# The maxima of the attention scores, reduced over two PSUM banks at a time

## The reference

```python
scores = einsum('bhqd,bhkd->bhqk', q, k) * scale     # 16 heads, 128 x 128 each
attn = softmax(scores, axis=-1)
y = einsum('bhqk,bhkd->bhqd', attn, v)
```

## Time and profile before

| what | us |
|---|---|
| median of 3 runs | 760.41 (759.85 to 762.28) |
| the profiled execution | 765.32 |
| its span, from first to last instruction | 763.6 |
| PE busy in the span | 687.0 (90%) |
| DVE busy in the span | 458.2 (60%) |
| all 256 reductions of line 576, busy | 164.3 |

### The profile page before, as it was taken

The page is one execution under the profiler, slowest core; times in us unless marked ns, Lnnn a source line. Parts: engine busy times, 40 slices in busy tenths (PEclk is TensorE's granted clock), DMA queues, the critical chain, the costliest instruction groups (busy, mean ns, idle before and its releaser), DMA issues. The chain is left out here.

```text
span 763.6 us, 19550 instructions
## 1 busy us (share of the span) xinstructions
PE 687.0 (90%) x6885; PEld 522.2 (68%) x6885; DVE 458.2 (60%) x1267; ACT 437.5 (57%) x679; POOL 299.6 (39%) x491
## 2 busy tenths in 40 slices
PE   5888999999969599899999999784899999997997
PEld 5646666666657377799999999771666666665553
DVE  6676887776654322533333444464899987775663
ACT  4346888888834133244444444452688889884442
POOL 5664545441142773573005720046766232112110
PEclk8979999999999899999999999996999999997999
DMA  6686665444112512133123331267454344400011
GB/s 206 103 147 105 133 131 115 103 103 74 36 31 63 199 45 70 49 108 93 55 70 88 108 94 40 68 145 139 106 121 123 83 77 82 69 2 1 29 42 42
DMA packets 72405, 66.77 MB, mean 87 GB/s; under 512 B 8159, under 2 KB 63352, under 8 KB 72056
## 3 DMA queue, kind: packets, MB, share of 16 engines
q1 hardware_dynamic: 57800, 51.88, 30.3%
q0 software_dynamic: 4096, 8.40, 3.9%
q10 hardware_dynamic: 10416, 5.25, 2.5%
HBM read 21.55 MB, written 16.65 MB: 50 GB/s over the span
## 5 line engine op out<-in xcount | busy, mean ns | idle before, releaser
L576 DVE TENSOR_REDUCE a_negmax<-psum 128x4 f32<-128x512 f32 x256 | 164.3, 684 | 7.0 <-PE psum L690 6.3
L443 ACT ACTIVATE temp<-psum 128x1024 f32<-128x1024 f32 x128 | 131.0, 1024 | 19.4 <-PE psum L708 13.2
L690 PE MATMUL psum<-a_k_stack,a_q_stack 96*128 96x256 bf16 x512 | 84.5, 283 | 6.2 <-DVE a_negmax L576 4.5
L722 PE MATMUL psum<-temp,a_v_st 128*18 128x128 f32 x2048 | 81.2, 275 | 7.2 <-issue 3.1
L1393 PE MATMUL psum<-f_w,f_h 128*128 x624 | 87.4, 284 | 0.0
L1380 PEld LDWEIGHTS psum<-f_bxT,f_bw 128*128 128x128 f32 x624 | 82.6, 193 | 6.5 <-issue 3.7
L1380 PE MATMUL psum<-f_bxT,f_bw 128*128 128x128 f32 x624 | 83.1, 277 | 3.3 <-DVE f_bw L1245 3.3
L1051 ACT ACTIVATE f_h<-psum 128x512 f32<-128x512 f32 x78 | 46.6, 597 | 62.2 <-PE psum L1380 62.2
L1245 DVE COPY f_bw<-f_w 128x512 f32 x78 | 34.1, 437 | 79.2 <-PE psum L1380 79.2
L708 PE MATMUL psum<-a_q_stack,a_k_stack 128*128 128x128 bf16 x1024 | 80.1, 222 | 0.7 <-ACT temp L443 0.3
L377 POOL CAST a_nm_cols<-a_negmax 128x16 bf16<-128x16 f32 x64 | 13.6, 212 | 170.9 <-DVE a_negmax L576 170.7
(11 more groups left out here) (204 smaller groups left out, 1258.2 us busy)
## 6 DMA issues: line engine op xcount, KB each, us to landing
a_k_stack<-a_k_parts SPq DMA_DIRECT2D x192, 64.0 KB
a_q_stack<-a_q_parts SPq DMA_DIRECT2D x96, 128.0 KB
xs<-zeros ACTq DMA_DIRECT2D x8, 640.0 KB, 5.2
f_w<-in_f_w SPq DMA_DIRECT2D x18, 256.0 KB, 4.5
scratch<-xs SPq DMA_DIRECT2D x18, 256.0 KB, 3.3
ys<-f_y_out SPq DMA_DIRECT2D x18, 256.0 KB, 2.3
scratch<-in_ctx SPq DMA_DIRECT2D x16, 256.0 KB
x<-in_x SPq DMA_DIRECT2D x8, 256.0 KB, 6.1
```

The costliest lines, as they stand in the source:

```text
L443: nc.scalar.activation(pt[:, unit].rearrange("p a b t -> p (a b t)"), ps[:, bank:bank + 2].rearrange("p a n -> p (a n)"), ACT.Exp, scale=S ...
L576: nc.vector.tensor_reduce(negmax[:, b % 2, :, 2 * unit:2 * unit + 2].rearrange("p n b -> p b n"), ps[:, P1_BANK + unit % 2].rearrange("p ( ...
L690: last = nc.tensor.matmul(ps[:, P1_BANK + unit % 2, 2 * j * P:2 * (j + 1) * P], q_cols(b, blk, STACK_ROWS), k_cols(b, blk, STACK_ROWS, sli ...
L722: last = nc.tensor.matmul(ps[32 * j:32 * j + V_COLS, PV_BANK, bass.ts(half, P)], v_st[:, b % 2, c0:c0 + V_COLS], pt[:, half, par, j], star ...
```

## The change

The four reductions of a step become two. Each reads both banks at once (1024 columns) and writes eight maxima a partition in place of four. The first waits for units 0 and 1, the second for units 2 and 3. The semaphore `negmax` now counts two a step, and the other waits on it (in `p1`, in `split`, in the second mixture's `up`) are counted anew. PE starts units 2 and 3 of a step when the reduction of units 0 and 1 has finished, and units 0 and 1 when that of units 2 and 3 of the step before has.

```diff
-                    def maxima(b, unit):
-                        dve.wait_ge(s["p1"], 4 * b + unit + 1)
-                        if unit == 0:
+                    def maxima(b, pair):
+                        dve.wait_ge(s["p1"], 4 * b + 2 * pair + 2)
+                        if pair == 0:
                             wait(dve, s["split"], b - 1)
-                        nc.vector.tensor_reduce(negmax[:, b % 2, :, 2 * unit:2 * unit + 2].rearrange("p n b -> p b n"),
-                                                ps[:, P1_BANK + unit % 2].rearrange("p (b n t) -> p b n t", b=2, n=2),
+                        nc.vector.tensor_reduce(negmax[:, b % 2, :, 4 * pair:4 * pair + 4].rearrange("p n b -> p b n"),
+                                                ps[:, P1_BANK:P1_BANK + 2].rearrange("p a (b n t) -> p (a b) n t", b=2, n=2),
                                                 AX, ALU.max, negate=True).then_inc(s["negmax"], 1)
...
                         if 0 <= t < B:
                             maxima(t, 0)
-                            maxima(t, 1)
                         if 0 <= t - 3 < B:
                             normalise(t - 3)
                         if 0 <= t < B:
-                            maxima(t, 2)
-                            maxima(t, 3)
+                            maxima(t, 1)
...
                     def p1(b, unit):
-                        wait(pe, s["negmax"], 4 * b + unit - 1)
+                        wait(pe, s["negmax"], 2 * b + unit // 2)
```

More of the change, by code:

```diff
@@ L374, in split @@
                         r = b % 2
-                        pool.wait_ge(s["negmax"], 4 * b + 4)
+                        pool.wait_ge(s["negmax"], 2 * b + 2)
                         wait(pool, s["nm_tr"], b - 1)
@@ L1648, in up @@
                 pe.wait_ge(f.s["w_folded"], 1)
-                pe.wait_ge(a["negmax"], 4 * B)
+                pe.wait_ge(a["negmax"], 2 * B)
             for blk in range(NB1):
```

## The result

The changed kernel takes 777.33 us (median of 4, 771.7 to 781.0) against 761.2 before; the ratio is 1.021 with a 95% interval of 1.014 to 1.027. Measured again beside the experiments, on another occasion, it took 775.48 us (median of 6) against 762.39, ratio 1.017 (1.014 to 1.021). So it is 13 to 16 us slower. The forecast was 12.6 us slower, 773.0, with a range of 766 to 780.

What follows compares the result with a forecast made beforehand. PE bounds most steps, the DVE some in the second attention, through the loop of units and reductions; 8.1 + 0.2 + 3.9 + 1.4 + 0.8 = 14.4 us, less what is taken off, leaves 12.6: 773.0 us, range 766 to 780.

Steps and rivals of the forecast that it cites:

- Length of a reduction: Line 576: 1024 columns take 1.215 us, saving 0.07 us a pair, 9 us of DVE time.
- rival 1: Reading two banks costs more: a reduction takes 1.29 to 1.364 us, the kernel 776.4 to 779.7 us; chance 0.13.
- The end of the second pair: Within a step, the second pair of units cannot end before 2.51 us from the step's start; 2.16 before.
- From the pair's end to the step: A delay of the second pair delays the step: 0.35 us without a piece between pairs, 0.30 with transposes.
- the 36 steps: 23 steps with no piece between the pairs, 8.1 us lost, and 13 with transposes between them, 3.9 us.
- The value steps: Steps with the value product between pairs: second pair starts 2.11 us behind the first, so loss 0.
- The steps bound by the DVE: Nine steps of the second attention: loss 0.14 us on PE, 0.16 on the DVE, 1.4 us in all.
- The DVE's busy time: Over the whole kernel, the DVE's busy time falls from 458 to about 450 us.
- The starts: First steps of both attentions, where four reductions lie end to end in the first step: 0.8 us lost.
- What was swallowed: Taken off: 0.3 us for a stall at 68 to 71 us, 0.9 for ACT's DMA waits in the second attention.
- rival 3: New idle time lowers PE's granted clock in a few stretches, 5 to 10 us more: 778 to 783; chance 0.05.
- Rival 4: Faster: the DVE's 9 us shorten the loop if a reduction takes 0.865 us; at best 751.4 us; chance 0.04.

Runs made afterwards that it cites:

- the kernels with the wait alone, on either side: Kernel before, four reductions: PE starts units 2 and 3 after both reductions (770.82 us, ratio 1.011), or each reduction waits for both units (771.11 us, 1.010).
- the kernel with 96 keys: Changed kernel with merged reductions over 96 of each head's 128 keys, 768 columns in place of 1024; 760.02 us, ratio 0.996 (0.994 to 0.999).
- the experiment: Kernel before with merged reductions only in steps t = 0 to 3 of both attentions; ratio 1.0035 (1.0006 to 1.0065), 2.7 us.

## Why the prediction was right, and where it was off

*The bound.* PE in most steps, the DVE in some of the second attention, and the loop of units and reductions inside a step: the kernels with the wait alone, on either side, show that this loop costs what it was said to cost without any merged instruction, and the kernel with 96 keys that no other part of the change costs anything that can be seen.

*Length of a reduction.* 1.215 was worked out, 1.226 measured. The price of a column taken from two other operations held: 768 columns took 0.958, so 256 columns more cost 0.268, 1.05 ns each. The ends that were kept for the range, 1.29 and 1.364, weren't needed; rival 1 is out.

*The end of the second pair.* 2.51 was the sum, 2.53 is the value of the trace, in every step without the value product. The start behind the units was 0.04 for 0.03, and the 0.06 from the DVE's end to PE was right.

*From the pair's end to the step.* This term was mis-sized. The prediction took 0.35 a step where no piece lies between the pairs, less 0.08 in the early ones, and 0.30 where transposes do. The two traces have 0.24 to 0.28 in the late steps (from 24 or 27 on) and 0.18 to 0.23 in all others. PE's rows before were said to lie end to end behind the second pair. They do by the rows' modelled ends, but the table has 2.18 from the pair's end to the next step before and 2.09 wherever the pair comes later. The slack lies ahead of `pv`: in the earlier trace rows `pv` starts 0.03 behind the pair's end (192.68), in the changed kernel 0.07 before it (197.19), and from the start of `pv` to the next step it is 2.16 and 2.15. What held `pv` there was not tried; it also waits for ACT's copy of the maxima (line 458), which ended at 192.43, 0.25 before, so that cause stays open. Over the 36 steps the sum had 11.4 us and the traces have about 8.3 (33 of them read, the three others taken at their neighbours' length): 3 us too much in the forecast.

*The value steps* were put at no loss. They kept 5.62 us in the first attention in every trace, and the kernel with merges only there is at 1.001 (0.998 to 1.004).

*The steps bound by the DVE.* 0.16 was worked out for the time from the first reduction's start to the last one's end, 0.19 is in the rows. The sign, which is the surprising part, was right: the engine without idle time got shorter reductions and took longer. Whole steps of this kind grew by 0.18 to 0.36 between the two traces.

*The DVE's busy time.* This sign was wrong: it was to fall from 458 to about 450 us and is 457.2. The shorter reductions are there, but not counted was that their starts overlapped the work ahead of them, 8.3 us before and 1.3 now.

*The starts.* This term was too small. 0.8 us was taken for both; the experiment has 2.7 (0.5 to 5.0). The prediction costed at nothing the wait of a step's first unit for the whole last reduction of the step before, since that reduction ends at 3.76 and the next step starts at 4.70. In the late steps that holds. In the first step of the second attention it doesn't: nothing else holds PE there for as long, it waits 1.32 us, and this one step is 1.6 us longer (0.4 with the first pair alone merged). The granted clock is 0.50 there and units take longer, which was not counted either; how much of the 2.7 us is due to that was not tried.

With the measured terms the sum is 8.3 for the 36 steps, about 1.7 for the nine bound by the DVE and 2.7 for the starts, 12.7 us, against the 13.3 measured beside the experiments. The forecast of 12.6 fits so well because 3 us too much and 2 us too little nearly cancel; that part is luck.

*What was swallowed.* Of the delays that were expected to fall into waits, no run separates the 0.9 us of ACT's waits for DMAs; one of those six waits, of 8.3 us, was nearly the whole 11.3. The other one was the stall of PE in the fifth step of the first attention. That step took 8.86 before and 8.66 in the changed kernel; in seven other traces that stall isn't there, and the step takes 5.2 to 6.4 us; in the remaining four it takes 8.1 to 10.0, so it comes and goes with either kind of reduction.

*The rivals.* The clock as a further cost of the change (rival 3) is not seen where steps are undisturbed: over 184 to 208 us of the changed kernel, the late steps, PE's granted clock is 1.00 with PE busy 22.30 of 24 us, and over 570 to 600 us it is 1.00 with 27.70 of 30.

```profile
184.00:208.00 24.00, 22.30 (x331) 15.83 (x335) 16.66 (x26) 18.55 (x27) 3.46 (x16) 1.00 0.20 57
```

Rival 4 named a point, 0.865 us for a reduction at which the pair keeps its end. With the slack the point is nearer to 0.95, and the kernel with 0.958 shows what lies behind it: even there only 0.4% are gained. Two single durations less the merged one are 0.14 us, but two back to back take 1.29, so 0.06 is what a pair gets back; and the engine as a whole got back 1.0 us for 128 instructions saved. The Trainium skill, "VectorE: DVE Perf Modes", section on the TRN2 errata, gives an instruction with a PSUM source a fixed 120 cycles at 0.96 GHz; an estimate from that is 0.125 us saved for each instruction, and this case doesn't bear it out. The other page's sentence (the Trainium skill, "Perfetto Trace Analysis", "Optimizing Scalar/DVE Operations": where an engine is not saturated but causes bubbles on others, breaking up instructions may let work end sooner) is this case, and the trace agrees with its 18.6 us of PE's waits.

## What to carry to other kernels

Two banks that take turns are worth their overlap and not their size: an instruction that reads both at once makes the two engines wait for each other in turn. Here 0.06 us saved a pair stands against a second pair of units that ends 0.37 us later. Before merging, add up the loop, from the producer's start over the merged reader to the producer's next start, and compare it with the gap that other work leaves there: 1.93 us was free of charge where the gap was 2.1, and cost up to 0.28 a step where it was 1.5. Do it for the first steps too, where the next step's first unit may be the one that waits. Of two such merges the one that nothing in the same step waits for cost 0.3% here (0.0 to 0.6%) and gained nothing. Whether two more banks for the units would keep the overlap with merged reductions was not tried.

## What the runs showed beside it

The scatter between runs of one kernel is some 10 us, and it comes in pieces that a single trace has or has not, whatever the reductions: the sixth step of the second attention (7.6 to 10.1 us), a stall of PE in the fifth of the first (5.2 to 10.0 us), and the last stretch behind the attentions, which took 79.8 to 81.1 us in most traces and 84.2 to 84.3 in three. In each of these three the granted clock falls to 0.65 to 0.68 over 20 us, where before had 0.89 (first the kernel in which PE waits for pairs, then before):

```profile
705.00:725.00 20.00, 19.09 (x58) 9.41 (x58) 11.12 (x47) 6.83 (x10) 2.40 (x4) 0.65 0.04 14
```

```profile
703.00:723.00 20.00, 18.95 (x81) 9.81 (x81) 13.86 (x58) 9.30 (x15) 3.60 (x6) 0.89 0.04 14
```

PE was busy 15.18 of the 20 us ahead of it in the first, and 15.39 in the second, so the rows don't say why one fell further than the other. Two traces of such kernels must be compared step by step before their spans are.
